# A different order for layer 0's last routings in a two-layer gated cross-attention kernel

## What is computed

```
x = x + tanh(g_xattn[0]) * L0_xattn(layernorm(x), ctx, ctx, fside, mask)
x = x + tanh(g_ffn[0])   * L0_ffn(layernorm(x))      # top 2 of 8 experts, capacity
x = x + tanh(g_xattn[1]) * L1_xattn(layernorm(x), ctx, ctx, mask)
x = x + tanh(g_ffn[1])   * L1_ffn(layernorm(x))      # top 2 of 8, dense, gated

# L0_ffn: n = 4096 tokens, cap = 1076 slots for each expert
probs = softmax(xf @ Wg); topv, topi = top_k(probs, 2)
pos   = sum(cumsum(one_hot(topi)) * one_hot(topi)) - 1     # rank of a token in its expert
dest  = where(pos < cap, topi * cap + pos, dropped)
buf[dest] = xf; y = gelu(buf @ W1 + b1) @ W2 + b2; out = y[dest] * gates
```

## Time and profile before

| | before |
|---|---|
| time, median of 3 runs | 926.21 us (925.9 to 927.81) |
| the profiled execution | 927.88 us, its span 926.1 us |
| mean granted TensorE clock | 0.956 of 2.4 GHz |
| busy: PE / DVE / ACT / POOL | 85% / 74% / 66% / 59% of the span |
| chain that ended last, by engine | PE 40%, DVE 25%, ACT 16%, issue 10%, POOL 8% |

### The profile page before, as it was taken

How to read it: one execution, slowest core, us unless ns; L and a number is a source line. 1 busy time by engine, 2 the same in 40 slices (tenths; PEclk the granted TensorE clock), 3 DMA queues, 4 the chain that set the end, 5 groups by cost and what they waited for, 6 DMA issues and landing times.

```text
span 926.1 us, 20429 instructions
## 1 busy us (share of the span) xinstructions
PE 784.4 (85%) x6554; PEld 618.1 (67%) x6554; DVE 688.7 (74%) x1980; ACT 609.3 (66%) x2582; POOL 546.6 (59%) x798
## 2 busy tenths in 40 slices
PE   2698999888964899998877788888978889999996
PEld 1366666666742799987555556656756768888885
DVE  5688899999987334454988799999887666666664
ACT  2498899889852445444976779799987444444442
POOL 6266578888677002031668887465324867777775
PEclk9999999999995799999987889999999999999998
DMA  6999975576248433225328365654100000000000
GB/s 165 242 268 242 261 244 145 120 172 155 57 108 300 126 108 96 71 80 122 80 65 160 101 126 133 147 121 125 47 14 23 24 23 24 24 23 13 12 1 23
DMA packets 85139, 101.68 MB, mean 110 GB/s; under 512 B 8448, under 2 KB 70853, under 8 KB 84360
## 3 DMA queue, kind: packets, MB, share of 16 engines
q1 hardware_dynamic: 80936, 92.13, 38.9%
q0 software_dynamic: 4096, 8.25, 3.6%
HBM read 63.32 MB, written 45.99 MB: 118 GB/s over the span
## 4 chain that ended last, share of the span: by engine, by line
PE 40%; DVE 25%; ACT 16%; issue 10%; POOL 8%; DMA 1%; SPq 0%; POOLq 0%; DVEq 0%; ACTq 0%
ACT exp L856 12%; PE psum L699 7%; DVE shift L1041 5%; PE psum L739 5%; PE psum L741 5%; PE psum L740 5%; DVE exp_T L1051 2%; PE psum L687 2%; DVE ln_stats L1023 2%; DVE exp_T L1053 2%; PE psum L688 2%; PE psum L689 2%; POOL scratch_xe L1568 2%; POOL got_rows L1587 2%; PE psum L582 2%
## 5 line engine op out<-in xcount | busy, mean ns | idle before, releaser
L856 ACT ACTIVATE exp<-psum,shift 128x120 f32<-128x120 f32 x1024 | 367.3, 441 | 72.8 <-DVE shift L1041 72.3
L856 ACT ACTIVATION_READ_ACCUMULATOR exp<-psum,shift 128x1 f32 x1024 | 276.2, 286 | 0.0
L569 PE MATMUL psum<-ident,exp 128*120 128x128 f32 x1024 | 162.3, 282 | 33.0 <-DVE exp_T L1053 18.0
L1041 DVE TENSOR_REDUCE shift<-psum 128x4 f32<-128x480 f32 x256 | 165.6, 648 | 28.6 <-PE psum L560 27.6
L1422 DVE SCALAR_TENSOR_TENSOR q_operand<-psum,comb,q_operand 128x256 f32<-128x256 f32 x256 | 111.5, 479 | 73.7 <-ACT q_operand L988 73.7
L1657 POOL TENSOR_TENSOR q_operand<-q_operand 128x512 f32<-128x512 f32 x96 | 126.4, 1317 | 58.7 <-DVE q_operand L1422 53.4
L569 PEld LDWEIGHTS psum<-ident,exp 128*120 128x120 f32 x1024 | 117.5, 141 | 52.5 <-DVE exp_T L1053 23.4
L988 ACT ACTIVATE q_operand<-psum 128x512 f32<-128x512 f32 x128 | 76.2, 599 | 114.7 <-PE psum L741 114.6
L1587 POOL DMA_INDIRECT got_rows<-scratch_y,slot_get x64 | 67.1, 1048 | 123.7 <-DMA scratch_y<-y_rows 107.2
L557 PE MATMUL psum<-neg_rows,const_bf 128*128 128x480 bf16 x256 | 98.0, 383 | 39.0 <-ACT exp L856 28.3
L560 PE MATMUL psum<-k_operand,q_operand 128*128 128x240 bf16 x512 | 97.3, 273 | 0.0
(11 more groups left out here) (175 smaller groups left out, 1669.8 us busy)
## 6 DMA issues: line engine op xcount, KB each, us to landing
k_operand<-scratch_k SPq DMA_DIRECT2D x32, 360.0 KB, 6.9
q_operand<-scratch_q SPq DMA_DIRECT2D x30, 384.0 KB, 6.4
scratch_q<-parts SPq DMA_DIRECT2D x15, 384.0 KB
scratch_k<-parts SPq DMA_DIRECT2D x14, 360.0 KB, 4.4
scratch_xe<-in_zero_rows SPq DMA_DIRECT2D x8, 512.0 KB, 8.5
scratch_y<-in_zero_rows SPq DMA_DIRECT2D x8, 512.0 KB, 6.7
scratch_q<-parts SPq DMA_DIRECT2D x15, 256.0 KB
scratch_k<-parts SPq DMA_DIRECT2D x14, 240.0 KB, 4.0
```

The source lines that it names most:

```text
L569: ins = pe.transpose(ps[0:S2, T_BANKS[G % 2], u * S:(u + 1) * S], atts[l].expS[:, G % RING_E, u, :], ident[:, :])
L856: ins = act.activation(atts[l].expS[:, G % RING_E, u, :], ps[:, S_BANKS[G % 3], u * S2:(u + 1) * S2], ACT.Exp, bias=atts[l].shift[:, i % 2 ...
L1041: dve.tensor_reduce(atts[l].shift[:, i % 2, 4 * r:4 * r + 4], ps[:, S_BANKS[G % 3], 0:4 * S2].rearrange("p (h k) -> p h k", h=4), AX_X, AL ...
```

## The change

Four things are done. Chunk 4 of layer 0 is given the short distances that chunks 5 and 7 have (`TIGHT0`: its sends are in slots 109 to 116, where they were in 117 to 124). Powers are done at distance 0 with `TIGHT0`, and in every slot the powers of all chunks stand ahead of everything else of the chunks' loop on GpSimd. Chunk 6 has a table of its own, `NEXT0`, with shorter distances still. And the key split of set 2 moves from distance 8 to distance 19, behind the last chunk's slots. The small mask for layer 1 is loaded and made some slots earlier.

```diff
-TIGHT0 = dict(stat=0, power=1, norm=4, turn=6, turned=7, gate=10, logits=13, top=13, one_hot=13, exp=14,
+TIGHT0 = dict(stat=0, power=0, norm=4, turn=6, turned=7, gate=10, logits=13, top=13, one_hot=13, exp=14,
               ranks=15, take_ranks=17, positions=17, slots=17, send=18)
+NEXT0 = dict(stat=0, power=0, norm=4, turn=5, turned=6, gate=8, logits=10, top=10, one_hot=10, exp=11,
+             ranks=11, take_ranks=13, positions=13, slots=13, send=14)
 def post_at(l, j):
-    return POST if j < 5 else TIGHT0 if l == 0 else TIGHT6 if j == NCH - 2 else TIGHT
+    return POST if j < 5 - (l == 0) else (NEXT0 if j == NCH - 2 else TIGHT0) if l == 0 else TIGHT6 if j == NCH - 2 else TIGHT
-SPLIT_KEYS_AT = {5: (0, 1), 8: (2,), 19: (3, 4, 5)}
+SPLIT_KEYS_AT = {5: (0, 1), 19: (2, 3, 4, 5)}
@@ GpSimd, behind(l, s)
-            if l == 0 and s == 124:
-                one_mask()
             if l == 0 and s % 16 == 2 and s // 16 + 1 < NCH:
                 masks(s // 16 + 1)
+            if l == 0 and s == 116:
+                one_mask()
+            for j in range(NCH):
+                if s - after_slot(j) == post_at(l, j)["power"]:
+                    powers(1, l * NCH + j)
             for j in range(NCH):
                 o = s - after_slot(j)
-                if o == post_at(l, j)["power"]:
-                    powers(1, l * NCH + j)
@@ SyncE, behind(l, s)
-            if l == 0 and s == 120:
+            if l == 0 and s == 110:
                 sp.dma_start(mask1[:], t["mask1"]).then_inc(mask_in, 16)
```

## The result

| | before | after |
|---|---|---|
| time, median | 926.06 us (924.28 to 927.81, 4 runs) | 942.22 us (941.66 to 944.23, 4 runs) |
| ratio, with its 95% interval | | 1.0176 (1.016 to 1.0192) |
| span of the profiled execution, mean clock | 926.1 us, 0.956 | 940.6 us, 0.944 |

The change makes the kernel 16.3 us slower by the ratio (16.2 by the medians). The forecast was 934.6 us, in a range of 928.3 to 938.5: slower was right, the size was half of what came.

What follows compares the result with a forecast made beforehand. No single bottleneck: layer 0's attention engines are all busy in a ring, with GpSimd's queue ahead of two normalisations mattering most. 2.5 + 4.9 - 0.9 + 1.6 + 0.3 = +8.4 us on 926.21 gives 934.6 us, range 928.3 to 938.5.

Steps and rivals of the forecast that it cites:

- what it costs to move the powers ahead of the sends: GpSimd's queue, layer 0: chunk 4's normalisation loses cover for a send's flight; chunk 5's powers only change places with a send.
- Chunk 4's normalisation, +2.5: Slot 95: normalisation waits for a bare send flight, delaying TensorE's transposes in slot 97; +2.5 us, ends 1.7 and 5.5.
- Ahead of slot 97: Layer 0's attention before chunk 4's transposes: the forecast had no term, so 0 us.
- Chunk 5's normalisation behind chunk 4's sends, 4.9 + 1.6 for the clock, 0.9 paid back: Slots 111 and 113: chunk 4's slots and three sends stall TensorE 4.9 us; half clock +1.6; earlier ranks and positions -0.9.
- The tail, 0 (-1.2 to +1.1) and +0.3 for the split: Last chunks: chunk 7's later normalisation and earlier logits cancel, 0 us; a key split beside chunk 7's sends +0.3.
- The key split, -1.2 and +0.3: VectorE, chunk 7: logits taken 1.2 us earlier without the split ahead; split beside chunk 7's sends costs 0.3 us.
- Weights and the last landing, 0: Later load of the last experts' weights may meet the last send's landing: 0, at most 2.4 us.
- More is lost: Rival, chance 0.06: both stalls halve the clock and the last landing meets the weights; +12.9 us, 939.1 us.
- The absorbing ring: Rival, chance 0.20: the engines' ring absorbs a part, only chunk 5's stall counts, clock stays; +4.3 us, 930.5 us.
- the waits: Sign: TensorE waits for `xn_rows` from GpSimd about 2 us in slot 97 and about 6 us in slot 113.
- without idle time: Sign: GpSimd goes without idle time from chunk 3's sends to chunk 5's normalisation, which ends near 245 us.
- the last maximum: Sign, told by layer 0's last exponential: at about 272 us instead of 264.3.

Runs made afterwards that it cites:

- e1: The changed kernel with chunk 4 put back on its former, longer distances, all other edits kept: 935.23 us, ratio 1.0089.
- e2: The kernel before with only chunk 4 moved to TIGHT0, its powers still behind the last send: 936.46 us, ratio 1.0113.
- e6: The changed kernel with only the powers put back behind the sends, at distance 1 in TIGHT0 and NEXT0: 940.57 us, ratio 1.0153.
- e5: The kernel before with only the powers of layer 0's post-attention normalisations moved ahead of the sends: 933.79 us, ratio 1.0063.
- e3: The changed kernel with only chunk 4's slots and sends moved behind chunk 5's normalisation: 939.15 us, ratio 1.0129.
- e4: The changed kernel with 11 and 22 extra matmuls ahead of TensorE's waits for chunk 4's and 5's normalised rows: 942.27 us, ratio 1.0165.
- e11: The kernel before with chunk 4 on TIGHT0 but its transposes and gate later (slot 100, gate distance 12), powers behind the sends: ratio 1.0061.
- e13: The kernel before with chunk 6 on NEXT0 and chunk 7's powers behind two of chunk 6's sends instead of four: ratio 0.9997.
- e7: The kernel before with only chunk 6's routing on NEXT0, powers at distance 1, behind four of chunk 6's sends: 932.79 us, ratio 1.0064.
- e8: The kernel before with only the split of key set 2 moved behind chunk 7's last ranks: 926.32 us, ratio 1.0001.
- e9: The kernel before with chunk 6 on NEXT0 but its sends from distance 18, behind chunk 7's powers: ratio 1.003.
- e10: The kernel before with chunk 4 on in-between distances: transposes in slot 100, slots and sends behind chunk 5's normalisation, powers as before: ratio 1.0019.

## Why the prediction was half right

The change as a whole can be put together from its parts: chunk 4 alone 10.5 us, powers ahead 5.8, the closer chunk 6 with its powers where the change has them about 0, the split about 0: 16.3 us, and 16.3 were measured. That it meets so closely is luck: the first part is known to 2.4 us and the second to 1.6, and e1 and e2, which halve the change, give 18.7. The parts also lie elsewhere in the changed kernel than alone, as follows.

The forecast had 8.1 us in the attention (its sum without the 0.3), and 15.1 were measured. By place: ahead of slot 97 2.1 for 0, at the first wait 6.0 for 2.5, at the second and behind it 7.0 for 5.6.

- **The step that failed: what it costs to move the powers ahead of the sends.** The forecast had 0.8 us for it at chunk 4's normalisation (2.5 taken, 1.7 of them even if the send landed at once), nothing ahead of slot 97, and nothing at chunk 5's: "Its own powers only change places with chunk 3's seventh send". e6 takes back this move alone, and its attention is 9.0 us late instead of 15.1: of the 6.1 us between, 1.8 arise ahead of slot 97, 3.3 at the first wait and until the second, 0.8 at the second and 0.1 behind. By itself the move costs 5.8 us (e5), most of it at chunk 5's normalisation. The argument that the forecast made for chunk 4, powers that covered a flight, holds for chunk 5 word for word, and was not made; it is why half of the loss stays without chunk 4 (e1). In the changed kernel itself that flight is covered by chunk 4's slots and sends, and the earlier powers show there as a wait of 2.55 us for VectorE's statistics.
- **Chunk 4's normalisation, +2.5: mis-sized, the place where most of that shows (6.0).** The mechanism was there to the letter: send, bare flight, normalisation. But the working itself gave 3.15, and 2.5 was taken because a lower end "rests on less"; the flight was 2.61 us instead of 2.17; and the clock was counted for the second wait alone, with the first as an upper end and a rival of 0.06. The wait itself is 4.5 us at the next maximum; e6, with the flight covered, has 2.4 there. What made 6.0 of the 4.5 until the next wait is open: the slow spell from 214 to about 221 us and chunk 4's gate and logits, which moved into it. In e2 0.8 us arise there at full clock, so the slow spell is not all of it.
- **Ahead of slot 97, nothing was forecast.** Moving powers ahead costs some 0.7 us there (e1, e3, e4, e5: 0.9 to 1.1 us at 204 us, against 0.0 to 0.3 without). How was not looked into; the other 1.1 of after's 2.1 are in its one profiled execution alone.
- **Chunk 5's normalisation behind chunk 4's sends, 4.9 + 1.6 for the clock, 0.9 paid back: right.** It is 5.7 us at the wait in e2, e6 and e11, 6.5 in after with the 0.8 for the powers, 0.5 more behind it, and 5.6 for it by itself with the payback (e11; 5.6 forecast). The Trainium skill ("TensorE: Matmul & The Clock Gate", Part 1, the HAM clock gate) says that the array drops to 1.2 GHz after an idle spell. The trace agrees, with 0.50 behind both of after's waits, and with the second wait filled the clock stayed at 1.00 (e4). What the clock cost at the second wait is 1.1 us (e4) for the 1.6.
- **The tail, 0 (-1.2 to +1.1) and +0.3 for the split: right for the sum, +0.9, and for a wrong reason.** The two sends ahead of chunk 7's powers were seen, and that they cost little holds (e13). Four would cost 5.9 us (e7), which the forecast didn't see. The powers' place, harmful for chunks 4 and 5, is what pays for the closer chunk 6: with the powers behind, the way is 41.7 us (e6). Of the 0.3 for a split beside the sends 0.1 is seen: chunk 7's eight sends start within 9.88 us (305.62 to 315.50) against 9.79 (289.39 to 299.18).
- **The key split, -1.2 and +0.3: not seen as a gain (e8).** The logits are taken without a split ahead, but the last send comes no sooner.
- **Weights and the last landing, 0: nothing contradicts it.** Most of the 1.8 us by which the later stages of the two profiled executions differ lies at the first expert: from the fetch of its rows to the first store 14.8 us (318.42 to 333.18) against 15.9 before (301.41 to 317.30), at a mean clock of 0.74 against 0.66 in the first 16 us. Why the clock differed wasn't tried, nor whether it does so in other executions.
- **The rivals.** "More is lost" had the half clock behind both waits, at 0.06, and stopped at 939.1, 3 us short, since it too took 2.5 for chunk 4's wait and nothing ahead of it. The absorbing ring was wrong: both waits show in full at the last maximum.

Of what was to show it, the waits (2 and 6 us forecast, 3.1 and 6.8 seen) and the tail (within 1 us) came; GpSimd was not without idle time, and the last maximum came at 277.5 where some 270 was expected.

## What to carry to other kernels

When work is moved out from between two instructions of which the second waits for the first's flight, the flight becomes bare: ask this of every instance that the loop makes, not only of the one that the change is about. A wait of TensorE of some 3 us in a full ring is paid, here with 2.7 to 4.5 us at the next maximum (e1, e5, after); the half clock behind it was the smaller part of the loss where it could be told apart (e4, and e2 against e6). Where the working of a term gives a number, that number is taken, and not a rounder one below it.

## What the runs showed of the hardware

Parts don't add up when they move within one in-order queue: the closer chunk 6 costs 5.9 us with chunk 7's powers behind four sends (e7) and nothing measurable behind two (e13, on another chip).

Two waits of TensorE of equal length, 1.59 and 1.60 us, at the same place of the program were followed by a clock of 1.00 in one kernel and of 0.50 in the other (e2, e6).

On two of the chips before took 948.4 and 945.3 us instead of 926. In a trace from there TensorE stops within a run of 32 matmuls on the values, for which everything is there, and no releaser is seen (e13's kernel):

```profile
231.21 0.27 PE L584 MATMUL psum<-exp_T,v_spread 120*32 120x128 f32 x1 [0.48 <-issue]
232.59 0.38 PE L584 MATMUL psum<-exp_T,v_spread 120*32 120x128 f32 x2 [1.12 <-issue]
```

The same 32 matmuls took 1.08 us in one piece in the traces of before and e7, from other chips. Such pauses stood at the same slots in the traces of several kernels from both chips (the lateness grows by 2.4 us at the 93rd maximum in e9, and by 2.3 to 2.4 in e10 to e13; between the 105th and 109th it grows by 4.3 us in e9). What they wait for the profile doesn't show.
